# A field-pair interaction kernel on one NeuronCore: 31 work units per batch chunk instead of 32, with rewritten orders on every engine

## The reference

```
e = stack([tbl_f[ids[:, f]] for f in range(32)], axis=1)            # 512 x 32 x 64
z[b, p] = sum_ij e[b, x_p, i] * w[p, i, j] * e[b, y_p, j]           # 512 x 496
h = concatenate([z, dense_ctx], axis=1)                             # 512 x 512
h = maximum(h @ W_top1 + b_top1, 0)                                 # 512 x 512
h = maximum(h @ W_top2 + b_top2, 0)                                 # 512 x 256
y = h @ W_top3                                                      # 512 x 1
```

## Time and profile before

| what | us |
|---|---|
| launch, median of 3 (lowest, highest) | 263.56 (263.34, 263.77) |
| span of the profiled execution, first to last instruction | 217.7 |
| launch less span: start and end, outside the profile | 45.9 |
| TensorE busy | 196.1 |
| VectorE busy | 174.1 |
| ScalarE busy | 150.4 |
| GpSimd busy | 150.2 |

### The profile page before, as it was taken

How to read it: one execution, slowest core, us unless ns; L and a number is a source line. 1 busy time by engine, 2 the same in 40 slices (tenths; PEclk the granted TensorE clock), 3 DMA queues, 4 the chain that set the end, 5 groups by cost and what they waited for, 6 DMA issues and landing times.

```text
span 217.7 us, 6053 instructions
## 1 busy us (share of the span) xinstructions
PE 196.1 (90%) x2072; PEld 131.6 (60%) x2072; DVE 174.1 (80%) x159; ACT 150.4 (69%) x1146; POOL 150.2 (69%) x186
## 2 busy tenths in 40 slices
PE   0029899699999989999999999999999999999985
PEld 0007553575758549556786556865677755767874
DVE  0003789679999999999998999979989989897911
ACT  2010268299799957998199896599959978999201
POOL 4777777777777777777777777777788718777300
PEclk9999999969999999999999999999999999999999
DMA  5666656667111111111111111111110000000000
GB/s 190 252 222 223 230 205 223 218 215 229 30 25 29 35 24 29 29 24 32 25 27 32 27 24 34 25 29 30 29 27 6 2 3 0 2 5 0 3 0 3
DMA packets 6432, 15.21 MB, mean 70 GB/s; under 512 B 2689, under 2 KB 2945, under 8 KB 5250
## 3 DMA queue, kind: packets, MB, share of 16 engines
q1 hardware_dynamic: 2306, 10.62, 13.7%
q0 software_dynamic: 4096, 4.20, 9.3%
HBM read 14.82 MB, written 0.00 MB: 68 GB/s over the span
## 4 chain that ended last, share of the span: by engine, by line
PE 79%; POOL 12%; issue 4%; DMA 3%; ACT 1%; DVE 0%; DVEq 0%
PE pu L485 25%; PE pu L477 24%; PE pz L498 13%; POOL emb L284 12%; PE pt L505 6%; PE pt L452 4%; PE pt L517 3%; DMA emb<-in_tbl,idx 3%; PE pu L505 1%; PE pt L527 1%; DMA idx<-in_ids 1%; PE pt L463 1%; PE pu L517 0%; ACT eT L303 0%; DVE zT L421 0%
## 5 line engine op out<-in xcount | busy, mean ns | idle before, releaser
L284 POOL DMA_INDIRECT emb<-in_tbl,idx x128 | 120.9, 945 | 41.1 <-issue 30.2
L312 ACT ACTIVATE turned<-turned 128x64 f32<-128x64 f32 x544 | 130.2, 245 | 1.5 <-DVE turned L389 1.5
L312 ACT ACTIVATION_READ_ACCUMULATOR turned<-turned 128x1 f32 x544 | 104.1, 191 | 0.0
L389 DVE TENSOR_TENSOR turned<-pu,emb 128x1024 f32<-128x1024 f32 x64 | 75.9, 1215 | 8.1 <-PE pu L477 7.8
L407 DVE TENSOR_TENSOR prod<-pu,eT 128x1024 f32<-128x1024 f32 x48 | 57.1, 1216 | 23.4 <-PE pu L485 23.3
L485 PEld LDWEIGHTS pu<-eT,ws 64*128 64x128 f32 x1024 | 64.9, 198 | 11.8 <-issue 10.4
L485 PE MATMUL pu<-eT,ws 64*128 64x128 f32 x1024 | 69.2, 287 | 0.0
L477 PE MATMUL pu<-ws,eT 64*128 64x512 f32 x256 | 65.5, 612 | 0.0
L303 ACT COPY eT<-pt 128x128 f32<-128x128 f32 (+1 forms) x28 | 11.2, 398 | 41.6 <-PE pt L452 41.6
L270 POOL TENSOR_TENSOR turned<-turned 128x512 f32<-128x512 f32 (+4 forms) x45 | 27.3, 607 | 11.4 <-DVE turned L389 8.4
L477 PEld LDWEIGHTS pu<-ws,eT 64*128 64x128 f32 x256 | 21.1, 186 | 16.7 <-issue 15.1
(11 more groups left out here) (24 smaller groups left out, 25.4 us busy)
## 6 DMA issues: line engine op xcount, KB each, us to landing
ws<-in_w SPq DMA_DIRECT2D x8, 1024.0 KB, 5.0
emb<-in_tbl,idx POOLq DMA_INDIRECT x128, 2.4
w1s<-in_w SPq DMA_DIRECT2D x1, 1024.0 KB
zT<-in_dense SPq DMA_DIRECT2D x1, 512.0 KB, 4.1
w2s<-in_w SPq DMA_DIRECT2D x1, 512.0 KB
idx<-in_ids SPq DMA_DIRECT2D x1, 64.0 KB, 1.8
identity<-in_ident SPq DMA_DIRECT2D x1, 64.0 KB, 1.8
w3s<-in_w SPq DMA_DIRECT2D x1, 1.0 KB
```

The source lines that it names most:

```text
L284: nc.gpsimd.indirect_dma_start(out=emb[:, c % EC, x, :], out_offset=None, in_=tables[x], in_offset=bass.IndirectOffsetOnAxis(ap=idx[:, c, ...
L312: i = nc.scalar.activation(t, t, ACT.Copy, accum_out=zB[:, b // NT % 2, b % NT * 16 + v:b % NT * 16 + v + 1])
L389: nc.vector.tensor_tensor(turned[:, b % RB, :, :].rearrange("p (x f) i -> p x (f i)", x=2), u.rearrange("p x s i -> p x (s i)"), e, ALU.mu ...
```

## The change

1. **31 units.** The four b units go. Four a units with other fields (`A_X`) and three new units c0, c1, c2 (`C_X`) cover the pairs inside the groups of eight fields, so that every unit is full (31 x 16 = 496) and the dense inputs get rows of z of their own. The c units have their eight small matmuls with the embeddings as the weights, like turned units. 15 units are summed now, 16 turned (13 four, 3 c).
2. **One list.** All of TensorE's work between steps, the sums too, stands in one table `PLAN`: after which step comes what. Layer 1 of a chunk is one piece instead of two.
3. **New orders.** `UNIT_ORDER` gives an order of units for each chunk, and `ROWS` and `Z_OUT` are new. ScalarE gets 37 row sums instead of 34, VectorE 18 instead of 21, GpSimd 9 as before.
4. **Groups of transposes.** The second chunk's sixteen field pairs are transposed in seven groups (4, 2, 2, 2, 2, 2, 2) instead of four of four.
5. **The end by block.** Layer 1 of the last chunk signals each of four blocks, layer 2 takes them as they come, and layer 3's two matmuls wait apart.

```diff
-    UNITS += [("a", 4 * _j + 3, 4 * _j), ("b", 4 * _j + 3, 4 * _j)]
+    UNITS += [("a", 4 * _j + 3, 4 * _j)]
+UNITS += [(_c, KP - 1, 0) for _c in C_X]
-XN = [1, 4, 4, 4]
+X_SIZES = [[1, 1, 1, 1, 1, 1, 1, 1, 1, 1, 1, 1, 1, 1, 1, 1],
+           [4, 2, 2, 2, 2, 2, 2],
+           [4, 4, 4, 4],
+           [4, 4, 4, 4]]
+PLAN = [(-1, 'x', 0), (-1, 'x', 1), (-1, 'x', 2), (-1, 'x', 3), (-1, 'x', 4), (1, 'x', 5), (1, 's', 0), (2, 'x', 6),
...
@@ products
+                if UNITS[u][0] in C_X:
+                    for slot in range(4):
+                        for bank in range(2):
+                            x = slot_of(u, bank, slot, 0)[0]
+                            rows = slice(EMB * (x % 2), EMB * (x % 2 + 1))
+                            i = nc.tensor.matmul(pu[:, unit_slot(t), bank, slot, :], eT[rows, c % EC, x // 2, :], ws[rows, u, slot, :],
+                                                 start=True, stop=True)
+                    i.then_inc(u_ready, 1)
+                    return
@@ TensorE's loop and end
-            for user in TURNS[-1]:
-                through_pt(*user)
-            for t in range(NS):
-                products(t)
-                for user in TURNS[t]:
-                    through_pt(*user)
-                for a in SUMS.get(t, ()):
-                    sums(a)
-            pt_free("l1a", last)
-            pe.wait_ge(mult_done, NS - 1)
-            layer1(last, (0, 2, 3, 1), Z_ORDER[:ZCH - ZA])
-            for a in SUMS[NS]:
+            for t in range(-1, NS):
+                if t >= 0:
+                    products(t)
+                for extra in TURNS[t]:
+                    also(*extra)
+
+            pe.wait_ge(pt_read, len(USERS))
+            layer1(last, 0, Z_ORDER[:ZCH - ZA])
+            pe.wait_ge(mult_done, NS - 2)
+            for n in (2, 3):
+                layer1(last, n, Z_ORDER[:ZCH - ZA])
+            pe.wait_ge(mult_done, NS - 1)
+            layer1(last, 1, Z_ORDER[:ZCH - ZA])
+            for a in range(len(SUMS), BCH * NA):
                 sums(a)
             pe.wait_ge(z_out, BCH)
-            layer1(last, range(N1), Z_ORDER[ZCH - ZA:])
-            through_pt("l2", last)
-            through_pt("l3", last)
+            for n in L1_LAST:
+                layer1(last, n, Z_ORDER[ZCH - ZA:]).then_inc(h1_last, 1)
...
+            pe.wait_ge(h2_act, 1)
+            nc.tensor.matmul(pt[0:1, 0, :], w3s[:, 0:1], h2[:, 0, :], start=True, stop=False)
+            pe.wait_ge(h2_dve, 1)
+            nc.tensor.matmul(pt[0:1, 0, :], w3s[:, 1:2], h2[:, 1, :], start=False, stop=True).then_inc(y_ready, 1)
```

More of the change, by code:

```diff
@@ L48 @@
 Z_ORDER = [z for z in range(ZCH) if z >= ZA] + list(range(ZA))
-assert NU == 32 and NT == 16 and all(UNITS[u][0] == "four" for u in TURNED)
+assert NU == 31 and NT == 16 and all(UNITS[u][0] != "a" for u in TURNED) and not any(UNITS[u][0] in C_X for u in SUMMED)
 assert ZCH * P == FIELDS * (FIELDS - 1) // 2 + DENSE
-TURN_AT = [TURNED, [5, 6, 7, 8, 9, 14, 16, 17, 18, 19, 20, 21, 22, 23, 26, 29], [2, 6, 7, 8, 9, 10, 14, 16, 17, 22, 23, 24, 26, 27, 28, 30], [0, 5, 9, 10, 11, 13, 14, 15, 18, 19, 20, 22, 23, 24, 25, 26]]
@@ L53 @@
[L53 to L64, removed]
@@ L115 @@
 WU = 4
+NW = -(-NU // WU)
 W_AT_ONCE = 2
-XN = [1, 4, 4, 4]
-GROUPS = [(c, k, XN[c]) for c in range(BCH) for k in range(0, KP, XN[c])]
-NG = len(GROUPS)
[L127 to L134, removed]
@@ new lines, with in_ring @@
+X_RING = (False, False, False, False)
+GROUPS = [(c, sum(X_SIZES[c][:i]), n) for c in range(BCH) for i, n in enumerate(X_SIZES[c])]
+NG = len(GROUPS)
+GROUP_OF = {(c, k + i): g for g, (c, k, n) in enumerate(GROUPS) for i in range(n)}
+def in_ring(g):
+    return X_RING[GROUPS[g][0]]
+L1_PARTS = {"l1a": (0, 1), "l1b": (2, 3), "l1": (0, 1, 2, 3)}
+PLAN = [(-1, 'x', 0), (-1, 'x', 1), (-1, 'x', 2), (-1, 'x', 3), (-1, 'x', 4), (1, 'x', 5), (1, 's', 0), (2, 'x', 6),
[13 rows of a table added]
+PLAN += [(Z_LAST, "z", BCH - 1)]
@@ new lines, with l1_place @@
+TURNS = {t: [v[1:] for v in PLAN if v[0] == t] for t in range(-1, NS)}
+assert [v[0] for v in PLAN] == sorted(v[0] for v in PLAN)
+assert [v[2] for v in PLAN if v[1] == "x"] == list(range(NG))
+SUMS = [v[2] for v in PLAN if v[1] == "s"]
+assert SUMS == list(range(len(SUMS))) and all(v[0] > STEP_A[v[2]] for v in PLAN if v[1] == "s")
+USERS = [v[1:] for v in PLAN if v[1] != "s" and not (v[1] == "x" and in_ring(v[2]))]
+PLACE = {v: i for i, v in enumerate(USERS)}
+def l1_place(c, i):
+    return next(PLACE[part, c] for part in L1_PARTS if i in L1_PARTS[part] and (part, c) in PLACE)
@@ L155, in dlrm_tower, with unit_slot @@
+RING = [v for t in range(-1, NS) for v in [("u", t)] * (t >= 0) + [v for v in TURNS[t] if v[0] == "x" and in_ring(v[1])]]
+TURN = {v: n for n, v in enumerate(RING)}
+NR = len(RING)
+PT_X = [g for what, g in USERS if what == "x"]
+RING_X = [g for what, g in RING if what == "x"]
+assert all(v[0] == "u" for v in RING[NR - UR:])
+def unit_slot(t):
+    return TURN["u", t] % UR
+Z_OUT = [30, 58, 88]
 def dlrm_tower(nc, tables, ids, w, dense, w1, b1, w2, b2, w3, ident, out):
@@ L191, in dlrm_tower @@
         s_emb = [sem(f"emb_in{i}") for i in range(BCH * KP)]
-        s_w = [sem(f"w_in{i}") for i in range(NU // WU)]
+        s_w = [sem(f"w_in{i}") for i in range(NW)]
         s_dense = sem("dense_in")
@@ L219, in cols, with x_copied @@
             return slice(c * P, (c + 1) * P)
-        def by_vector(c, n, of):
-            return c == last and n >= of // 2
+        def x_copied(engine, c, k):
+            if not X_RING[c]:
+                engine.wait_ge(pt_read, PLACE["x", GROUP_OF[c, k]] + 1)
+            else:
+                engine.wait_ge(xr_read, RING_X.index(GROUP_OF[c, k]) + 1)
+        L1_LAST = (0, 2, 1, 3)
         def l1_out(c, n):
@@ L325, in layer1 @@
                     act.wait_ge(h2_ready, c)
[L326 to L327 removed]
+                for n in ns:
+                    i = nc.scalar.activation(h1[:, n, :], pt[:, n, :], ACT.Relu, bias=b1s[:, n:n + 1])
                 i.then_inc(pt_read, 1)
```

292 lines of the change are left out of this document (173 added, 119 removed), and 13 rows, old and new, of the table PLAN.

## The result

The changed kernel's launches take 261.98 us (median of 20, 260.89 to 264.69), those of the kernel before, run beside them, 263.65 us (median of 20). The ratio is 0.9949, with a 95% interval from 0.993 to 0.9968: faster, by some 1.7 us and not by the 5.3 forecast, and above the range's upper end of 261.5. The profiled launch took 264.56 us with a span of 262.8; launch less span is 1.76 us in that launch, and 1.75 to 1.94 in every later launch here, of either kernel.

What follows compares the result with a forecast made beforehand. TensorE was taken as the bound from the last gather it waits for: 196.8 + 1.5 clock + 1.8 waits = 200.1 against 205.5, end +0.1, so -5.3 us from 263.56 to 258.3, range 255.1 to 261.5.

Steps and rivals of the forecast that it cites:

- the first step of the sum: Launch time outside the profiled 217.7 us span: 45.9 us, taken as unchanged by the change.
- The wait for pair 13: First chunk: TensorE idles 1.98 us for this field pair's gathers before the change; the 2.0 us were to go.
- the idle time moved to pair 9: First chunk, between pairs 7 and 9: up to 2.9 us of TensorE idle time move there, 2.5 expected.
- the prices of the prediction: TensorE's time per piece: summed unit 0.89 us, turned 0.86, c unit 0.89, sum 0.43, layer 1 in one piece 3.76.
- Work, 3.3 us less from pair 9 on: TensorE's list from pair 9 to the last z transpose: 167.9 us of work before, 164.6 after.
- Idle time and clock, 2.0 us less: From pair 9 on: pair 13's 2.0 us wait goes; 1.5 us lost by lower clock and 1.8 by short waits stay.
- The end, +0.1: After the last z transpose: waiting for z's copy, five sums in one piece, layer 3 split; +0.1 us, between -0.3 and +0.6.
- ScalarE sets the pace: Rival, chance 0.20: ScalarE filled 97%, TensorE waits 4 to 5 us for its copies instead of 1.8; 260.5 to 261.5 us.
- c units that don't overlap: Rival, chance 0.06: their row halves run one after the other, 1.78 us each, 10.7 us more; 269.0 us.
- gathers that land late: Rival, chance 0.04: chunk 1's last pairs land at 84.0 us, wanted at 86.1; costs up to 1.2 us more, 259.5.
- VectorE as the bound: Rival, chance 0.07: VectorE's emptying of PSUM, 1.13 us a unit, holds TensorE in stretches; 1.5 us more, 259.8.
- signs named as wrong: Profile signs: c unit above 1.2 us, ScalarE copy waits over 3 us, chunk 1 gather wait, different time outside the span.

Runs made afterwards that it cites:

- e1: The kernel before, run again with no edit: 260.26 us (one launch), span 258.5.
- e7: The kernel before, with first-chunk gathers of pair k waiting until TensorE has transposed pair k-2: 269.82 us, 1.0258.
- e10: The changed kernel with 32 plain loads from SyncE in place of the first chunk's gathers: 230.12 us, 0.8734 of before.
- e9: The kernel before with 32 plain loads from SyncE in place of the first chunk's gathers: 231.74 us, 0.8797 of before.
- e2: The changed kernel, run again with no edit: 258.06 us (one launch), span 256.3.
- e3: The kernel before with only the first two of eight bilinear weight pieces loaded: 260.98 us, 1.0009 of before.
- e4: The changed kernel with only the first two of eight bilinear weight pieces loaded: 258.68 us, 0.9946 of before.
- e5: The kernel before with all weight loads issued at the start, not paced by the gathers: 261.18 us, 1.0029.
- e6: The changed kernel with all weight loads issued at the start, not paced by the gathers: 258.78 us, 0.9895 of before.
- e11: The changed kernel with six of ScalarE's 37 row sums given to VectorE: 263.8 us, 1.0003 of before.
- e15: The changed kernel, run again as it is, beside two variants on the same chip: 259.13 us, 0.9862 of before.

## Why the prediction was wrong

**What failed is the first step of the sum**, "I take the 45.9 us outside as unchanged". The sum was made against the one profiled span of 217.7 us, and that launch was unlike the timed ones. The kernel before has taken 258.6 to 265.4 us in every launch since, with less than 2 us of it outside the span wherever the span is on record. The landing, the waits and the clock that the sum starts from are those of the unlike launch. The wait for pair 13, the lower clock behind it and the idle time moved to pair 9 are no part of a launch that stands still past all of chunk 0's landings.

**Where the 40.8 us between the two spans of before are.** Windows cut at VectorE's first multiply of each chunk; first the trace shown ahead of the prediction, then the launch of the same kernel here (e1), from the restart on:
```profile
19.30:68.30 49.00, 46.10 (x472) 29.81 (x474) 42.93 (x37) 33.86 (x269) 37.12 (x40) 0.97 0.49 158
68.30:113.70 45.40, 44.72 (x478) 30.16 (x472) 43.85 (x40) 35.75 (x271) 34.43 (x37) 1.00 0.15 28
113.70:162.10 48.40, 48.40 (x538) 31.83 (x536) 45.06 (x41) 39.55 (x307) 36.52 (x40) 1.00 0.14 28
162.10:205.90 43.80, 43.80 (x496) 30.02 (x498) 39.45 (x36) 37.40 (x293) 29.45 (x55) 1.00 0.01 3
```
```profile
50.00:98.00 48.00, 44.57 (x433) 26.37 (x437) 40.12 (x35) 33.95 (x266) 28.27 (x31) 0.96 0.13 29
98.00:148.30 50.30, 47.77 (x490) 31.46 (x482) 44.23 (x41) 38.13 (x290) 30.23 (x32) 1.00 0.11 22
148.30:202.90 54.60, 50.67 (x525) 33.27 (x524) 45.45 (x40) 37.78 (x288) 30.29 (x32) 1.00 0.11 21
202.90:246.70 43.80, 43.80 (x496) 30.01 (x498) 39.47 (x36) 37.41 (x293) 29.19 (x54) 1.00 0.01 3
```
The second chunk starts 29.7 us later (98.0 against 68.3), the second and third take 4.9 and 6.2 us longer, and the last one, in which no gather is issued, takes 43.80 both times. So this is not a slower chip; it goes with the gathers, in all chunks. The quiet trace issues the same gathers, 1.25 us apart, without it. One handover shows how. In the trace shown first, a turned unit ends on TensorE at 158.48 + 1.13 = 159.61 and VectorE takes it 0.05 us later:
```profile
158.48 1.13 PE L477 MATMUL pu<-ws,eT 64*128 64x512 f32 x4
...
159.66 1.22 DVE L389 TENSOR_TENSOR turned<-pu,emb 128x1024 f32<-128x1024 f32 x1 [0.77 <-PE pu L477]
```
In e1 a summed unit ends at 169.84 + 1.16 = 171.00, and VectorE has done the multiply before it at 170.53 + 1.22 = 171.75. It starts on that unit (`prod`) at 173.21, 1.46 us after it was free. GpSimd had just issued four gathers in a row, the last two of them shown, and its next one, at 173.44, waits for the same signal: it is the sixteenth gather of the last chunk, which stands behind the 80th unit, and that is this unit.
```profile
169.84 1.16 PE L485 MATMUL pu<-eT,ws 64*128 64x128 f32 x16
...
170.53 1.22 DVE L389 TENSOR_TENSOR turned<-pu,emb 128x1024 f32<-128x1024 f32 x1
173.21 1.23 DVE L407 TENSOR_TENSOR prod<-pu,eT 128x1024 f32<-128x1024 f32 x1 [1.46 <-PE pu L477]
```
```profile
169.77 0.94 POOL L284 DMA_INDIRECT emb<-in_tbl,idx  x1 [0.30 <-issue]
171.02 0.95 POOL L284 DMA_INDIRECT emb<-in_tbl,idx  x1 [0.30 <-issue]
173.44 0.95 POOL L284 DMA_INDIRECT emb<-in_tbl,idx  x1 [1.48 <-PE pu L477]
```
Two engines that wait for one signal of TensorE go on within 0.23 us of each other, 2.2 us and more after the unit's end. So the signal came late to both, and it was not one engine that was slow to answer. Some of TensorE's signals are late so in e1 while gathers run back to back, but not all: ScalarE's copy of z at 170.15 follows the end of its transpose by 0.24 us. That the long stop is the same lateness, grown over the row of the first gathers, would fit but isn't shown. That a row of gathers is needed for the stop is shown (e7 to e10); that it isn't enough, the quiet trace shows. What else it takes is open. Every trace here but the one shown first keeps fewer records of semaphores: 1,610 updates in e1, and 1,905 in e9, which has late signals but no stop, against 3,112; and of the 16 updates that tell of a weight piece's landing, e1 has 1 to 7 for each piece between 19 and 41 us, against 13 to 16. So writing the records may be what the signals queue with. The Trainium skill, page "NOTIFIC — the notification-queue block", section "3. Interfaces", says that this unit can hold back the engines whose records it takes when a queue or one of its internal buffers is full; the thinned records would agree with it, and no run here, all of them recorded, can show it.

**What the change itself did.** The same windows for the changed kernel (e2), against the four above:
```profile
50.00:98.90 48.90, 44.41 (x480) 27.71 (x478) 34.59 (x32) 32.21 (x253) 28.34 (x31) 0.97 0.13 28
98.90:150.80 51.90, 47.76 (x511) 30.99 (x511) 44.32 (x40) 42.88 (x335) 30.31 (x33) 1.00 0.11 23
150.80:203.10 52.30, 50.21 (x537) 34.97 (x537) 45.34 (x41) 44.43 (x347) 31.54 (x33) 1.00 0.11 22
203.10:244.60 41.50, 40.95 (x460) 29.23 (x458) 37.64 (x33) 38.44 (x302) 27.75 (x53) 1.00 0.01 2
```
Chunk by chunk it is +0.9, +1.6, -2.3 and -2.3: 196.7 us become 194.6, and the end 11.8 becomes 11.7. The first of these is no loss by itself, since at 50 us e2 is at its third unit and e1 at its fifth. For the others the lists, cut at TensorE's first unit of each chunk, and the prices of the prediction give an estimate: 45.6 us becoming 43.4 in the second chunk, 48.4 becoming 47.0 in the third, 44.1 becoming 42.0 in the last. The trace shown first took 45.4, 48.4 and 43.8, so the prices hold where nothing is late. In e1 and e2 the last chunk gains what they say and the third more; it is the second, +1.6 in place of -2.1, that takes the gain back.

The prediction's terms start at pair 9. From its transpose to the last z transpose, first e1 and then e2:
```profile
58.60:246.28 187.68, 177.80 (x1857) 116.64 (x1859) 162.07 (x143) 142.56 (x1099) 113.40 (x143) 1.00 0.09 18
58.10:244.23 186.13, 175.59 (x1897) 117.77 (x1895) 157.37 (x139) 156.83 (x1230) 114.92 (x145) 1.00 0.09 18
```
The stretch shrinks by 1.5 us and not by 5.4; in the traces of e3 and e4, e5 and e6, e9 and e10 by 1.7, 1.3 and 0.3. Most of e10's 1.6 us lies ahead of pair 9, which TensorE transposes at 27.6 us in e9 and at 26.5 in e10.

- *Work, 3.3 us less from pair 9 on:* the prices hold piece by piece and in the last chunk, but TensorE's busy time falls by 2.2 us only (177.80 to 175.59), and by 1.1, 1.9 and 0.7 in the three other pairs of traces. Busy time isn't work alone here: in the trace shown first the same stretch of the kernel before is busy for 170.6 us, in e1, with less of the lower clock, for 177.8.
- *Idle time and clock, 2.0 us less:* wrong, 0.7 us more (9.9 to 10.5), and between 0.5 less and 0.6 more in the other pairs. There was no wait for pair 13 to save. That the new order needs the others' answers sooner in the second chunk, so that late signals cost it more, would fit but isn't shown.
- *The end, +0.1:* -0.1, inside its bounds.
- *ScalarE sets the pace (chance 0.20, 260.5 to 261.5):* nearest in time and, in e2's chain, ScalarE has 13%. But in the first trace of after it is busy for 132.3 us of the 159.9 from the end of the second chunk's first transposes (90.8 us) to the last z transpose, 83% and not 97%: the 134 us of work were right, the stretch was longer. Freeing 23 us of ScalarE gained nothing (e11).
- *c units that don't overlap, gathers that land late, VectorE as the bound:* not seen.
- Of the signs named as wrong, waits of the chain for ScalarE (3.83 and 6.59 us at 117 and 124 us) came true, and the one against which I set no chance at all: a different time outside the span.

What stays open is what the second chunk loses in the new order; moving row sums (54.4 us for that chunk) and merging transposes (51.5 to 51.7, against 51.9 and 52.0 in e2 and e15) did not find it.

## What to carry to other kernels

Hold the profiled span against the timed launch before anything else: a gap of 45.9 us with no row in it is a sign that the profiled launch was not one of those that were timed, and a second profile of the unchanged kernel settles it. Where the prices are right and the time is not, cut windows at the same program point and set what the sum gives for each beside it: that shows the chunk that loses, while busy time can differ for the same instructions (170.6 and 177.8 us here). An engine that dominates the waits is not the cause until work taken off it gives time back.

## What the runs showed of the hardware that was not expected

- While GpSimd issued some 30 gathers 1.25 us apart, TensorE, VectorE and ScalarE all but stood for about 25 us, in every trace here in which the first chunk is gathered so, but for the one shown ahead of the prediction. The two without gathers in that chunk (e9, e10) had no stop, and their launches were 12 to 13% shorter.
- Pacing the gathers moved the loss and did not remove it: 269.8 us for the kernel before with the second chunk left to catch up (263.05 unpaced), 261.0 for the changed kernel with all of them paced.
- A free VectorE took up a unit 0.05 us after its end on TensorE in the quiet trace; in e1, in the same kernel, it stood for 1.46 us more with the unit done.
- Two or eight weight pieces, early or paced by gathers, made no difference to the stop: 260.98, 261.18 and 260.52 us for the kernel before.
- The column of the granted clock does not show every stretch at the lower level. It reads 0.50 in e2 from 26 to 52 us and 1.00 all through e15 (third column from the end of its window, in which TensorE did nothing for 22 us). Yet in both a summed unit takes 2.08 us and a transpose 0.47 right after the stop, and in e15 1.16 and 0.33 some microseconds later:
```profile
26.00:48.00 22.00, 0.00 (x0) 0.00 (x0) 0.00 (x0) 0.00 (x0) 13.83 (x15) 1.00 0.60 198
...
49.38 2.08 PE L585 MATMUL pu<-eT,ws 64*128 64x128 f32 x16 [24.00 <-ACT eT L360]
51.40 0.47 PE L545 MATMUL pt<-identity,emb 128*128 128x128 f32 x1
...
54.56 0.33 PE L545 MATMUL pt<-identity,emb 128*128 128x128 f32 x1
...
55.51 1.16 PE L585 MATMUL pu<-eT,ws 64*128 64x128 f32 x16
```
